# Moving the first chunk's normalised rows and the block sums to the end of the second chunk, with two buffers put into memory freed from the DMA scratch

## The reference

```python
x = L0_attn_x                                   # (1, 2048, 512) float32
xn = _layernorm(x, axis=-1)
# attention block, on xn
x_norm = (xn - mean(xn)) / sqrt(var(xn) + 1e-5) * gamma + beta
q, k, v = x_norm @ qkv[:, :512], x_norm @ qkv[:, 512:1024], x_norm @ qkv[:, 1024:]
attn = softmax(where(causal, q @ k.T / sqrt(512), -inf))
a = attn @ v @ o_proj + xn
# gated feed-forward block, also on xn
h = silu(xn @ w_gate) * (xn @ w_up)             # (1, 2048, 2048)
h = keep the 2 largest of each 4 neighbours by magnitude
out = x + a + h @ w_down
```

## Time and profile before

| | |
|---|---|
| time, median of 3 runs (lowest, highest) | 793.25 us (792.91, 793.26) |
| span of the profiled execution | 791.1 us |
| PE busy | 787.2 us, 3560 matmuls |
| PE weight loads | 653.1 us |
| DVE busy | 606.0 us |
| ACT busy | 316.9 us |
| DMA | 121.75 MB, 154 GB/s in the mean |
| granted TensorE clock | 1.000 in the mean |

### The profile page before, as it was taken

One profiled execution on the slowest core, in us unless ns is written; L12 is line 12 of the kernel. 1 busy time (PEld: TensorE's weight loads), 2 busy tenths in 40 slices (PEclk: granted clock), 3 DMA queues, 4 the chain that ended last, 5 costly groups with the idle time before them and its releaser, 6 DMA issues.

```text
span 791.1 us, 9390 instructions
## 1 busy us (share of the span) xinstructions
PE 787.2 (100%) x3560; PEld 653.1 (83%) x3560; DVE 606.0 (77%) x979; ACT 316.9 (40%) x514; POOL 10.7 (1%) x23
## 2 busy tenths in 40 slices
PE   9999999999999999999999999999999999999998
PEld 6888888888888888888888888888888888888887
DVE  6978787477644797789989789798658658559786
ACT  5423222235122464464634634363424334335431
POOL 2010101000000000000000000000000000000000
PEclk9999999999999999999999999999999999999999
DMA  9541462300131524586454452697277163161002
GB/s 321 184 161 64 136 241 89 112 28 0 54 94 41 211 119 175 170 310 240 186 174 173 186 165 128 245 351 288 100 259 269 57 239 117 70 240 53 1 1 106
DMA packets 31612, 121.75 MB, mean 154 GB/s; under 512 B 3088, under 2 KB 3664, under 8 KB 29136
## 3 DMA queue, kind: packets, MB, share of 16 engines
q1 hardware_dynamic: 29120, 116.90, 40.2%
q10 hardware_dynamic: 2448, 4.26, 1.7%
HBM read 77.07 MB, written 44.07 MB: 153 GB/s over the span
## 4 chain that ended last, share of the span: by engine, by line
PE 99%; DMA 1%; SPq 0%; DVE 0%; issue 0%
PE bank L969 13%; PE bank L971 13%; PE bank L970 13%; PE bank L689 10%; PE bank L687 10%; PE bank L688 10%; PE bank L840 8%; PE bank L1049 7%; PE bank L1051 7%; PE bank L1050 7%; DMA raw<-L_attn_qkv 1%; PE bank L762 0%; PE bank L795 0%; PE bank L697 0%; PE bank L1062 0%; PE bank L1061 0%
## 5 line engine op out<-in xcount | busy, mean ns | idle before, releaser
L969 PE MATMUL bank<-X_hi,wset 128*128 128x512 f32 x448 | 174.6, 390 | 0.0
L971 PE MATMUL bank<-X_hi,wset 128*128 128x512 f32 x448 | 174.5, 389 | 0.0
L970 PE MATMUL bank<-X_lo,wset 128*128 128x512 f32 x448 | 174.5, 389 | 0.0
L971 PEld LDWEIGHTS bank<-X_hi,wset 128*128 128x128 f32 x448 | 84.1, 188 | 17.5
L969 PEld LDWEIGHTS bank<-X_hi,wset 128*128 128x128 f32 x448 | 84.1, 188 | 17.4 <-issue 0.2
L970 PEld LDWEIGHTS bank<-X_lo,wset 128*128 128x128 f32 x448 | 84.1, 188 | 17.3
L1049 PE MATMUL bank<-dw,hs_hi 128*128 128x512 f32 x224 | 87.4, 390 | 0.0
L1051 PE MATMUL bank<-dw,hs_lo 128*128 128x512 f32 x224 | 87.3, 390 | 0.0
L1050 PE MATMUL bank<-dw,hs_hi 128*128 128x512 f32 x224 | 87.2, 389 | 0.0
L1694 DVE TENSOR_TENSOR acc<-bank,acc 128x512 f32<-128x512 f32 x59 | 40.2, 688 | 40.1 <-PE bank L1051 39.6
L1049 PEld LDWEIGHTS bank<-dw,hs_hi 128*128 128x128 f32 x224 | 42.1, 188 | 8.9 <-DVE acc L1694 0.2
(11 more groups left out here) (263 smaller groups left out, 1491.0 us busy)
## 6 DMA issues: line engine op xcount, KB each, us to landing
w_operands<-wset SPq DMA_DIRECT2D x8, 3584.0 KB, 14.0
wset<-w_operands SPq DMA_DIRECT2D x8, 3584.0 KB, 11.4
wsum<-w_units SPq DMA_DIRECT2D x28, 256.0 KB, 3.6
dw_raw<-L_ffn_w_down SPq DMA_DIRECT2D x14, 512.0 KB, 5.0
xw<-L_attn_x SPq DMA_DIRECT2D x4, 1024.0 KB, 9.6
xt_raw<-x_t SPq DMA_DIRECT2D x8, 512.0 KB, 7.5
xn_t<-xt_raw SPq DMA_DIRECT2D x8, 512.0 KB, 2.8
acc<-resid SPq DMA_DIRECT2D x2, 2048.0 KB, 10.2
```

Of the source, the lines that this page charges most:

```text
L969: pe.matmul(dst[:], u[:, 0, :], x_hi, start=(first and kt == 0), stop=False, skip_group_check=True)
L970: pe.matmul(dst[:], u[:, 0, :], x_lo, start=False, stop=False, skip_group_check=True)
L971: last = pe.matmul(dst[:], u[:, 1, :], x_hi, start=False, stop=(kt == 1), skip_group_check=True)
```

## The change

Two steps move, two tiles get places of their own, and two waits go and one comes.

```diff
-              4: [x_scale[2], v[1][2], row_turn[2], row_copy[2], row_store[2], *xn[0], row_spread[2], xn_store[0]],
-              5: [v[1][3], xh_pre[2][0], ("block_sum", 0, 0)],
+              4: [x_scale[2], v[1][2], row_turn[2], row_copy[2], row_store[2], row_spread[2]],
+              5: [v[1][3], xh_pre[2][0]],
               6: [xh_pre[2][1], xh[2][0], xh_pre[2][2], xh[2][1], xh[2][2]],
-              7: [x_scale[3]]}
+              7: [x_scale[3], *xn[0], xn_store[0]]}
...
-    steps += [*u[0:2], ("rows_store", OLD - 1, 0), row_turn[3], row_copy[3], row_store[3], row_spread[3], *u[2:4], xn[2][0], ("rows_load", OLD + 1, 0),
+    steps += [*u[0:2], ("rows_store", OLD - 1, 0), row_turn[3], row_copy[3], row_store[3], row_spread[3], ("block_sum", 0, 0), *u[2:4], xn[2][0], ("rows_load", OLD + 1, 0),
...
-                  for c, pair in enumerate(((112, 116), (16, 20), (24, 28), (120, 124)))]
+                  for c, pair in enumerate(((112, 116), (208, 212), (24, 28), (120, 124)))]
...
+        spread0_rows = at("spread0_rows", 216 * KB, [P, 2, W], F32)
...
-            return spread[c][:, row:row + 1, :].broadcast_to((P, 2, W))
+            return (spread[c] if c else spread0_rows)[:, row:row + 1, :].broadcast_to((P, 2, W))
...
-                    if n == 2 and k == 0:
-                        act.wait_ge(blocks_stored, 64)
...
                     if u == 3:
+                        if c == WIDE[0]:
+                            dve.wait_ge(blocks_stored, 64)
...
-                    if n >= 2 and k == 0:
-                        dve.wait_ge(xn_ready[0 if n == 2 else 2], 2)
+                    if n == 3 and k == 0:
+                        dve.wait_ge(xn_ready[2], 2)
...
-    nc = bacc.Bacc("TRN2", target_bir_lowering=False, num_devices=1)
+    nc = bacc.Bacc("TRN2", target_bir_lowering=False, num_devices=1, dynamic_dma_scratch_size=1024)
```

More of the change, by code:

```diff
@@ L552, in _ @@
                     if n == 1:
-                        sp.dma_start(spread[0][:, 0:2, :], row_stats_dram[0, 0:2].rearrange("v t p -> v (t p)").partition_broadcast(P)
+                        sp.dma_start(spread0_rows[:], row_stats_dram[0, 0:2].rearrange("v t p -> v (t p)").partition_broadcast(P)
                                      ).then_inc(spread0_loaded, 16)
```

## The result

| | before | changed |
|---|---|---|
| time, median of 4 runs | 793.25 us (792.91 to 793.86) | 803.52 us (803.33 to 804.12) |
| ratio, 95% interval | | 1.0129 (1.0115 to 1.0144) |
| span of the profiled execution | 791.1 us | 801.8 us |
| mean granted TensorE clock | 1.000 | 0.994 |

The changed kernel is 10.3 us slower. The forecast was 798.1 with a range to 800.0: the sign and the place were right, the size (4.9 us) was under half of what came.

A forecast was written before the change was run, and what follows sets the result against it. PE was taken to bound the kernel, busy 787.2 of 791.1 us with no later waits. Nothing gained plus 4.9 us of DVE lateness gave 796.0, with 2.15 outside the span 798.1 us, range 795.0 to 800.0.

The forecast's parts named there:

- Steps 1 and 2: Tile 7 onward: chunk 0's `xn` ends about 141.6 us, its stores land at 144.5, block sums run 144.5 to 149.4.
- Step 5: DVE before the third maximum: 8.78 us of work after `blocks_stored`, so the maximum comes at 164.1, 4.9 us late.
- the chain: Around 165 us: PE needs unit 11's copy, behind ACT's third `xh`, which waits for DVE's third `xh_pre`; 4.9 us late.
- Step 4: Block stores, issued from 145.8 us behind the spread, wait for it; 2.36 MB at 406 GB/s, `blocks_stored` full at 155.3.
- a slow spread: Rival: chunk 3's spread takes 6.5 us, not 4.9, from traffic beside it; everything 1.6 us later, 799.7; chance 0.12.
- the likeliest case: The block stores queue behind the spread, DVE and then PE come 4.9 us late: 798.1 us; chance 0.57.
- The clock was a rival: Rival: PE, broken up near 166 us, falls to half speed for about 3.2 us, costing 1.6 more: 799.7; chance 0.07.
- The last of my own signs of being wrong: The prediction is wrong if PE's starts after 171 us are further apart than 0.23 us.
- Both slow cases at once: Slow spread (0.12) and falling clock (0.07) together, left outside the range of 795.0 to 800.0 us.
- Not slower: Rival: the last block store lands near 150.8 us, DVE 0.4 us late, 793.7, no change; chance 0.08.
- a gain: Rival: the kernel gets faster, which would need a PE wait taken away; no mechanism known; chance 0.02.

The follow-up runs named there:

- e3b_warm_from_start: Changed kernel plus 31 matmuls that serve nothing, 18 ahead of PE's wait for chunk 3's first `xT` half, 3 and 10 ahead of z's second and third matmul: 801.42 us.
- e2b_warm: Changed kernel with block sums and stores ahead of chunk 3's statistics store and spread, plus 1, 3 and 11 useless matmuls in PE's three gaps: 797.42 us.
- e4_places_only: Kernel before with only the new places, smaller scratch and changed waits, all steps where they stood: 793.34 us, ratio 1.000.
- e1_max_apart: Changed kernel, but `max_pair2` lies at 216 KB and DVE waits for `blocks_stored` only ahead of `max_one2`: 793.34 us, ratio 0.9998.
- e6_spread_alone: Changed kernel, but SP issues the first block store only after chunk 3's spread has landed: 802.16 us, ratio 1.0112.
- e7_stores_by_act: Changed kernel, but ACT issues the four block stores on its own queue instead of SP: 802.88 us, ratio 1.0122.
- e2_sums_first: Changed kernel, but the block sums and their stores stand ahead of the store and spread of chunk 3's row statistics: 799.06 us, ratio 1.0069.
- e5_xn_early: Changed kernel, but `xn` of chunk 0 and its stores stay at tile 4 and the block sums stand at tile 7: 793.13 us, ratio 0.9996.
- e3_warm_pe: Changed kernel plus 26 useless matmuls, 18 and 8 ahead of z of chunk 3's first and third matmul, behind PE's wait for the first `xT` half: 804.60 us.

## Why the prediction was wrong in its size

**What held.** PE had no reserve at 165.5 us; the lateness of DVE at the third maximum passed to PE one for one. With the clock kept up this can be read twice, each time against 159.17 and less what the execution was late by itself at PE's last score matmul (165.35 before). In e3b_warm_from_start DVE's third maximum started at 167.86, 8.3 us late (less 0.37), and the time was 8.3 us over before (801.42 - 793.08). In e2b_warm it started at 164.02, 4.3 us late (less 0.56), and the time was 4.3 over (797.42 - 793.08). That the places, the scratch and the dropped waits are worth 0 us is shown by e4_places_only, that the work taken from tiles 4 and 5 is, by e1_max_apart. Steps 1 and 2 were right to 0.1 us once the 0.38 us of this execution are taken off. Step 5's 8.78 us of DVE work measured 8.75 (167.66 - 158.91). The waits came in three pieces, the last ending where forecast in the chain.

**Step 4 failed: `blocks_stored` at 155.3.** It came at 158.9, or 158.5 without the 0.38. The 3.2 us too many are:

- 0.3: the row statistics landed in 2.1 us and not 1.8, so the spread was issued at 145.7.
- 1.3: the spread took 6.2 us and not 4.9. I had this as a rival of its own, "a slow spread", with 0.12. e6_spread_alone and e7_stores_by_act show what makes it slow: stores outstanding behind it on either queue. As the block stores are always issued there, this was not a rival but part of the likeliest case; the 6.5 us of the earlier trace rows with two stores behind was the row to take.
- 1.6: from the spread's landing (151.9) to the last store's (158.9) it was 7.0 us, where I had 5.4 (5.8 for 2.36 MB at 406 GB/s, less 0.4). The bulk was through by 157.3, just these 5.4 us. What was left is seen in the DMA window from 157.3 to 158.6 us:

```profile
DMA packets 8, 0.03 MB, mean 22 GB/s; under 512 B 1, under 2 KB 1, under 8 KB 8
```

Eight packets in 1.3 us, seven of them 4 KB packets of the stores, one behind the other with nothing else moving: the work of one DMA engine that had fallen behind. The wait ended only when the last of them was down. One instruction load of 16 KB ran in this stretch, in the window from 151 to 152.5 us:

```profile
q8 instruction: 1, 0.02, 3.9%
```

3.9% of 16 engines for 1.5 us is 0.94 us on one engine, most of the tail's length. Other runs fit. In e2_sums_first such a load ran between 147 and 149 us, among the stores, and they had the tail shown there. In e5_xn_early none ran among the stores, which landed in 2.9 us. In e6_spread_alone it ran between 150 and 151.5, as the first store was being issued, and from 157.1 on only this was left:

```profile
DMA packets 6, 0.01 MB, mean 9 GB/s; under 512 B 4, under 2 KB 4, under 8 KB 6
```

No run moves the load alone, and no view names the engine it ran on; it stays argued.

That the stores wait for the spread was right, the reason that I gave was not: it isn't that they stand behind it on the same queue. By e7_stores_by_act they wait nearly as long on another queue, for the DMA engines. And I took the wait as one-sided, with a spread as fast as alone.

**The clock was a rival with 0.07 and happened.** Its price was near, its chance was not. Worked out as 1.6 us, it measured 1.9 in the trace (6.48 - 4.58), 2.1 as the difference of e3b_warm_from_start to the changed kernel, and 1.6 on e2_sums_first. That the price came near is in part luck. I had taken 3.2 us at half speed with PE at work all through. The clock was low from about 169 to 179 us, three times as long, but for the first half of that PE mostly waited; what it cost is some ten starts 0.43 us apart instead of 0.227, 2.0 us. I thought of it as a sum on top, when the forecast itself had PE wait for 5 us in pieces. e2_sums_first, with DVE some 4 us late, still had the fall; so at the 4.9 us that I forecast it was to be expected, and the likeliest case should have had it in. The Trainium skill ("TensorE: Matmul & The Clock Gate", section "HAM oscillation — how this bites in real kernels") had said that gaps bring the lower clock; the trace agrees (0.50 from 170.3 to 179.4). It speaks of long gaps; in e2_sums_first the clock fell with three gaps, the longest 2.4 us.

The last of my own signs of being wrong, starts further apart than 0.23 us behind 171 us, is this: they were 0.43 apart.

Together: 4.9 + 3.2 + 2.0 = 10.1 us of the 10.3 measured. Both slow cases at once was what I left outside the range; they were not independent chances but both the usual course.

**Not slower** and **a gain** are refuted for this kernel as written; e1_max_apart shows what was needed for the first, and that even then there is no gain: 793.34 us is the kernel before. No run here beats it (the lowest, e5_xn_early at 793.13, isn't told from it).

## What to carry to other kernels

A tile that takes the place of a DMA's source waits for that DMA's landing, and the landing must be read as it will be in company: from a row with the same neighbours, the slowest engine included, not from the lone transfer or from bytes over bandwidth. Here another 4 KB place made the difference between 10.3 us and nothing. Where TensorE never waits, look for the engine that meets it with no reserve; each microsecond of wait brought in there counts in full, and once PE is broken up as it was here, the restart at half speed belongs into the sum, not among the rivals.

## What the runs showed of the hardware that was not expected

- A 1 MB broadcast load landed in 4.6 to 5.0 us with nothing issued behind it (e5_xn_early, e6_spread_alone), and in 6.2 to 6.3 with stores outstanding, whether these were on the same queue (changed kernel, e1_max_apart) or on another (e7_stores_by_act). Its 8 KB packets took 0.55 us each instead of 0.33, while no packet of the stores moved.
- The last of four stores landed over a microsecond after nearly all their bytes were down: the last seven 4 KB packets came one behind the other in 1.3 us (changed kernel).
- PE's clock fell to half although it did some work in between: in e2_sums_first PE was busy 0.99 of 4.40 us, with no wait over 2.4. In e3_warm_pe it still read 1.00 through a wait of 3.93 us and fell right behind it. Matmuls that serve nothing kept it up and made the kernel 2.1 us faster (e3b_warm_from_start against the changed kernel).
